# TensorE's order in the attention stage: the waits of two score groups put together, the value products behind the scores

## The reference, cut to what matters

```python
def attn(x, w_q, w_k, w_v, w_o):            # x: (16, 256, 256) f32, 16 heads of 16 features
    q, k, v = proj(w_q), proj(w_k), proj(w_v)
    scores = einsum('bhqd,bhkd->bhqk', q, k) * SCALE
    probs = softmax(scores)                 # over the 256 keys
    return einsum('bhqk,bhkd->bhqd', probs, v) ... @ w_o.T
x = layernorm(x + attn(x))
# then 8 experts, 2 for each of the 4096 tokens, at most 1280 tokens an expert:
#   gates, lists of tokens, relu(buf @ w1 + b1) @ w2 + b2, weighted sum
x = layernorm(x + ffn(x))
```

## Time and profile before

| | us |
|---|---|
| three runs | 1002.49, 996.72, 1003.08 (median 1002.49) |
| the profiled execution | 998.63 |
| its span, from the first to the last instruction | 996.9 |
| the stretch in which both score groups run in each turn | 76 to 376 |
| the experts' stretch at full work | 484 to 950 |

### The profile page before, as it was taken

The page is one execution under the profiler, slowest core; times in us unless marked ns, Lnnn a source line. Parts: engine busy times, 40 slices in busy tenths (PEclk is TensorE's granted clock), DMA queues, the critical chain, the costliest instruction groups (busy, mean ns, idle before and its releaser), DMA issues. The chain is left out here.

```text
span 996.9 us, 19588 instructions
## 1 busy us (share of the span) xinstructions
PE 841.5 (84%) x7441; PEld 754.0 (76%) x7441; DVE 560.8 (56%) x1125; ACT 460.5 (46%) x851; POOL 443.8 (45%) x674
## 2 busy tenths in 40 slices
PE   4559999999999987620699999999999999999940
PEld 4446777776777765520699999999999999999940
DVE  3345767776777774421456555456665655556415
ACT  3016656665666665201344444454444434454316
POOL 2001122555666556775334444445454444445325
PEclk9569989999999999755699999999999999999985
DMA  2967556777664640101424325233443433322229
GB/s 89 266 99 108 86 98 123 118 116 116 110 100 88 119 77 24 44 22 37 147 32 92 91 43 128 44 85 86 90 88 50 109 69 86 86 43 43 28 36 328
DMA packets 71225, 90.77 MB, mean 91 GB/s; under 512 B 10940, under 2 KB 62300, under 8 KB 71004
## 3 DMA queue, kind: packets, MB, share of 16 engines
q1 hardware_dynamic: 53724, 68.48, 31.5%
q0 software_dynamic: 17408, 21.05, 12.8%
HBM read 37.87 MB, written 25.84 MB: 64 GB/s over the span
## 5 line engine op out<-in xcount | busy, mean ns | idle before, releaser
L953 POOL DMA_INDIRECT acc_rows<-o_w,lists x80 | 136.8, 1710 | 242.6 <-ACT o_w L1004 230.4
L626 DVE TENSOR_REDUCE negm<-wide 128x4 f32<-128x1024 f32 x128 | 156.3, 1221 | 72.6 <-PE wide L728 71.0
L1082 PE MATMUL wide<-g_hi,w_hi 128*128 128x256 f32 x640 | 184.3, 288 | 0.0
L1084 PE MATMUL wide<-g_hi,w_lo 128*128 128x256 f32 x640 | 181.1, 283 | 0.0
L1083 PE MATMUL wide<-g_lo,w_hi 128*128 128x256 f32 x640 | 180.8, 283 | 0.0
L1101 PE MATMUL bank<-w_lo,h_hi 128*128 128x256 f32 x640 | 180.1, 281 | 0.0
L1100 PE MATMUL bank<-w_hi,h_hi 128*128 128x256 f32 x640 | 180.1, 281 | 0.0
L1102 PE MATMUL bank<-w_hi,h_lo 128*128 128x256 f32 x640 | 179.8, 281 | 0.0
L994 ACT ACTIVATE h<-wide,b1T 128x256 f32<-128x256 f32 x320 | 133.2, 471 | 70.8 <-DVE h_hi L1037 53.1
L473 ACT ACTIVATE probs<-wide 128x1024 f32<-128x1024 f32 x128 | 131.1, 1024 | 73.9 <-PE wide L742 70.3
L1004 ACT ACTIVATE o_w<-o_b,lists 128x256 f32<-128x256 f32 x80 | 36.3, 501 | 193.5 <-DVE o_b L1050 193.5
(11 more groups left out here) (143 smaller groups left out, 1518.3 us busy)
## 6 DMA issues: line engine op xcount, KB each, us to landing
stack<-qk SPq DMA_DIRECT2D x64, 256.0 KB, 7.1
w_raw<-in_L_ffn_w SPq DMA_DIRECT2D x16, 1024.0 KB, 5.8
stack<-qk SPq DMA_DIRECT2D x64, 128.0 KB, 5.9
x_sb<-in_L_attn_x SPq DMA_DIRECT2D x16, 256.0 KB, 4.7
x_rows<-x SPq DMA_DIRECT2D x16, 256.0 KB, 3.5
acc_rows<-x SPq DMA_DIRECT2D x16, 256.0 KB, 4.3
acc_sb<-acc_rows SPq DMA_DIRECT2D x8, 512.0 KB, 7.9
out<-out_sb SPq DMA_DIRECT2D x8, 512.0 KB, 3.7
```

What stands on the lines that cost most here:

```text
L626: nc.vector.tensor_reduce(negm[n % 2][:, :, :, u].rearrange("p c x -> p x c"), SQ[:, :, :].rearrange("p x (c t) -> p x c t", c=QC), X, ALU ...
L953: nc.gpsimd.indirect_dma_start(out=acc_d, out_offset=bass.IndirectOffsetOnAxis(ap=lists[:, e, QC * c + r, 0:1], axis=0), in_=o_w[c][:, r, ...
L1082: nc.tensor.matmul(out, w1_hi[:, k, f], G_hi[:, k, :], start=(k == 0), stop=False)
L1084: ins = nc.tensor.matmul(out, w1_lo[:, k, f], G_hi[:, k, :], start=False, stop=(k == DK - 1))
```

## The change

The waits of `scores` and `shifted_scores` become functions of their own, called one after the other in front of both groups; the value products of the turn follow right behind the two groups, ahead of `MT`, `UT`, `AT`, `X1T` and `POS`, where they stood behind these. No instruction is added or taken out, no buffer and no offset changes; the programs of the other engines are untouched.

```diff
--- before.py
+++ after.py
@@ -715,13 +715,24 @@
                     lambda i: src_hi[:, i, c * P:c * P + P], lambda i: src_lo[:, i, c * P:c * P + P],
                     lambda i: wT_hi[:, w, i, :], lambda i: wT_lo[:, w, i, :]))
 
-            def scores(n, u):
-                st, i = stack[n % SB], PAIRS * n + u
+            def scores_due(n, u):
+                i = PAIRS * n + u
                 if i == 0:
                     pe.wait_ge(b1T_done, 1)
                 if u == 0:
                     pe.wait_ge(stacked[n % SB], 128 * (n // SB + 1))
                 pe.wait_ge(max_done, i)
+
+            def shifted_scores_due(n, u):
+                i = PAIRS * n + u
+                if i == 0:
+                    pe.wait_ge(keys_ready, 16 * 2 * SB)
+                if u == 0:
+                    pe.wait_ge(shift_in, 64 * (n + 1))
+                pe.wait_ge(exp_done, i)
+
+            def scores(n, u):
+                st = stack[n % SB]
                 for c in range(QC):
                     for x in range(2):
                         k = slice(HALF * x, HALF * x + KEYS)
@@ -730,12 +741,7 @@
                 ins.then_inc(s_ready, 1)
 
             def shifted_scores(n, u):
-                st, i = stack[n % SB], PAIRS * n + u
-                if i == 0:
-                    pe.wait_ge(keys_ready, 16 * 2 * SB)
-                if u == 0:
-                    pe.wait_ge(shift_in, 64 * (n + 1))
-                pe.wait_ge(exp_done, i)
+                st = stack[n % SB]
                 for c in range(QC):
                     for x in range(2):
                         k = slice(HALF * x, HALF * x + KEYS + 2)
@@ -760,12 +766,19 @@
                 ins.then_inc(pv_ready, 1)
 
             for turn in range(LAST + 1):
-                p = pair_of(turn, S0, NB)
-                if p is not None:
-                    scores(*p)
-                p = pair_of(turn, ST0, NB)
-                if p is not None:
-                    shifted_scores(*p)
+                ahead, behind = pair_of(turn, S0, NB), pair_of(turn, ST0, NB)
+                if ahead is not None:
+                    scores_due(*ahead)
+                if behind is not None:
+                    shifted_scores_due(*behind)
+                if ahead is not None:
+                    scores(*ahead)
+                if behind is not None:
+                    shifted_scores(*behind)
+                for t in range(QUADS):
+                    m = due(turn, PV0 + 2 * t, NB)
+                    if m is not None:
+                        pv(m, t)
                 n = due(turn, MT, NB)
                 if n is not None:
                     pe.wait_ge(max_done, PAIRS * (n + 1))
@@ -814,10 +827,6 @@
                         nc.tensor.matmul(out, tri[:, :], mask[:, c, :], start=True, stop=False)
                         ins = nc.tensor.matmul(out, ones[:, :], (seen[m % 2], seen_t)[c][:, :], start=False, stop=True)
                     ins.then_inc(pos_ready, 1)
-                for t in range(QUADS):
-                    m = due(turn, PV0 + 2 * t, NB)
-                    if m is not None:
-                        pv(m, t)
                 n = due(turn, Q, NB)
                 if n is not None:
                     pe.wait_ge(xT_lo_done, n + 1)
```

## The result

| | us |
|---|---|
| the kernel before, median of 18 runs | 1002.02 (996.72 to 1009.75) |
| the changed kernel, median of 18 runs | 1010.46 (1004.96 to 1016.61) |
| ratio, with its 95% interval | 1.0081 (1.0059 to 1.0102) |
| profiled execution, before and after | 998.63 and 1014.60 |
| its span, before and after | 996.9 and 1012.8 |

The change costs 8.4 us by the two medians, 8.1 by the ratio. The two profiled executions are 16 us apart, one from the lower part of its kernel's runs and one from the upper: their stretches can't simply be subtracted.

The account below looks back on a forecast made before the run. TensorE, busy 841.5 of 996.9 us, was taken to bound the kernel. The terms 6.9 - 1.2 + 0.5 = +6.2 us, on a mean of 1000.2 us over four executions, gave 1006 us, range 997 to 1014.

Parts of the forecast that it names:

- UT behind the value products: Turn 3's eight transposes end later, delaying VectorE's division and MT in turn 4: 0.55 us a steady round, +6.9 us in all.
- POS behind them: Turn 7's four small matmuls next to V save one passage between array layouts: 0.1 us in 12 rounds, -1.2 us.
- AT behind them: Turn 5's four transposes still end before ScalarE's `aT_hi` reads them, 0.3 us to spare: cost 0, at most 0.5.
- waits in front: Both score groups' waits ahead of the scores: 0.05 to 0.1 us in ten turns, +0.5 us, bounds 0 and 2.
- The cover by the one subtraction: In turn 4 VectorE's 0.68 us `qk` subtraction before the reciprocals takes 0.45 of the 1.00 us delay; 0.55 gets through.
- The forecast wait of `MT`: Sign in turn 4: MT's wait for VectorE's line 568 grows from 0.2 to about 0.8 us in nearly every round.
- the three special rounds: Rounds outside the ten steady ones: late stack rows 0.2 us, slightly late scores 0.5, last turn 3 but one 0.7.
- The bound of 14.3: Upper bound for moving turn 3's transposes: all of the 1.02 us gets through in 14 rounds, 14.3 us.
- Nothing arrives: Rival: longer rounds give late stack rows time, so other stalls shrink by turn 4's loss; 998 to 1001 us, chance 0.15.
- Faster: Rival: the wait ahead of the shifted scores' weights was a hurdle; 0.11 us less in 117 turns, 985 to 993, chance 0.06.
- Slower by over 1%: Rival: one more wait ahead of the scores costs 0.1 us in each of 117 turns, above 1017 us, chance 0.16.
- the forecast's own range: Range of the main case: 999 to 1012 us, from 4 to 9 us on a base between 996 and 1003, chance 0.63.

Follow-up runs that it names:

- experiment 10: Kernel before with only the eight transposes of turn 3 (UT) behind the value products, on a chip without the hold: 1.0056 of the kernel before.
- experiments 6: The changed kernel unaltered, run again for a profile on the same chip as the kernel before: 1.0092 of the kernel before.
- 7: Changed kernel with only AT, the four transposes of turn 5, put back ahead of the value products: 1.0064 of the kernel before.
- experiment 11: Kernel before with only the waits of both score groups in front, value products in their old place, without the hold: 1.0052 of the kernel before.
- experiment 9: Changed kernel with UT, the transposes of turn 3, ahead of the value products again, on a chip without the hold: 1.0038 of the kernel before.
- experiment 2: Changed kernel with UT, the transposes of turn 3, ahead of the value products again, on the chip with the hold: 1.0338 of the kernel before.
- experiment 5: The kernel before unaltered, run again for a profile: 1.0007 against itself.
- experiment 1: Kernel before with only the eight transposes of turn 3 (UT) behind the value products, first chip: 0.9942 of the kernel before.
- experiment 8: Changed kernel with UT ahead of the value products and GpSimd's four list transfers one turn later, on a chip without the hold: 1.0211 of the kernel before.

## Why the prediction was right, step by step

The forecast was 1006 us with a range of 997 to 1014; 1010.5 came. By parts, on chips without the hold:

| part | forecast, us | measured, us |
|---|---|---|
| UT behind the value products | +6.9 | +5.6 (3.1 to 8.1; experiment 10) |
| POS behind them | -1.2 | turn 7 shorter by 0.09 to 0.1 in each round |
| AT behind them | 0 | not to be told from 0 (experiments 6, 7) |
| waits in front | +0.5 | +5.2 (2.4 to 8.0; experiment 11) |
| all but UT | -0.7 | +3.8 (1.0 to 6.6; experiment 9) |
| whole change | +6.2 | +8.1 (5.9 to 10.2) |

The measured ones are ratios times the median beside them. 5.6 and 3.8 make 9.4, which lies within the interval of the whole, so nothing speaks against adding the two halves.

- *UT in turn 3.* Right in place and size. The cover by the one subtraction gave way as worked out: 0.55 forecast, 0.52 measured in each steady round. The forecast wait of `MT` of about 0.8 is 0.73 in the row. Experiment 10 has it in ten rounds, as many as were counted. What the three special rounds cost can't be read beneath the late stack rows there. The bound of 14.3 was never near.
- *AT in turn 5.* Right where signals come in time: the trace of the changed kernel has the four transposes end at 267.52 and ScalarE's `aT_hi` start at 267.88, with no wait, and turn 6 keeps 3.29.

```profile
266.86 0.66 PE L702 MATMUL bank<-ident,attn 128*128 128x128 f32 x4
...
267.88 0.58 ACT L511 ACTIVATE aT_hi<-bank 128x512 fp32r<-128x512 f32 x1
```

But I called that cover 0.3 us wide and priced its loss at 0.5 at most. On the chip with the hold a kernel with the same place of `AT` (experiment 2) lost 2.3 us in turn 6 and 1.5 in turn 7 of each round. The bound was read from a trace in which signals are quick.
- *POS in turn 7.* Right: 0.1.
- *Both waits in front.* Mis-sized: +0.5 forecast within 0 to 2, +5.2 measured. The step priced each wait at the turn where it stands and found nothing, and in the steady turns that is so: the score groups stay 0.34 apart (259.30 to 259.64). Two things are missing from it. First, it said of the scores that wait for `shift_in` that TensorE loses nothing; in experiment 11 turn 86 lost 1.15 us to that wait, and turns 70 and 102 lost 0.25 each. Second, it left out that the edit changes what is issued at all, and with that turns 142 to 148, in which no scores are left. 2.5 us are found there in the mean of seven profiles, 4.7 in that of experiment 11, most of it with the lower clock. How the other 2.7 divide between the waits for the maxima, the clock elsewhere (from 76 us to the end of turn 149 it is at 1.2 GHz for 30.6 us in experiment 11, 13.6 in experiment 5 and 17.0 in the first profile of the kernel before) and what differs from run to run stays open.

The rivals. *Nothing arrives*: wrong, the steady loss is repaid nowhere. *Faster*: wrong, the shifted scores follow the scores by 0.34 us as before, so the 0.11 us are no hurdle that the order of the waits could take away. The first half of the Trainium skill's rule (TensorE: Matmul & The Clock Gate, Part 3) would have given the 13 us. With the second, that loads overlap matmuls in flight only where they go to another row group, the unchanged distance agrees; but no run had score groups on other rows, and the profile shows the loads of the shifted scores start at 259.52, while the matmuls of the scores (259.30 and 0.50, ends modelled) are in flight on the same two row groups. So whether that rule is the reason stays open. *Slower by over 1%*: its mechanism, 0.1 us a turn, is wrong, since six of eight turns kept their length; of its direction some was right, by another way. What the forecast owes to luck: UT was put 1.3 us too high and the waits 4.7 too low, and the base of four executions, 1000.2 in the mean, was 1.8 under the median of 18 runs. The errors stayed inside the range because it was made for runs that differ by more than the change. The 1% that I said a measurement can't tell was too coarse: with 18 runs of each kernel the interval is 0.2% to either side. And 4 us on a base of 996 make 1000, not the 999 at the lower edge of the forecast's own range.

## What to carry to other kernels

Ask of an edit in the order of waits not only what each wait delays but whether the waits still fit where they were: two in front of one instruction became 89 more instructions here, and most of the price that was found lay in turns that the edit does not reorder. When work moves behind other work, follow its reader to the next thing that waits for it and look for what covers it: one subtraction of 0.68 us took 0.45 of 1.00, and the rest went through one for one. And take a ratio of half a per cent on more than one chip before a sign is believed: UT alone was 0.994 on one and 1.006 on another.

## What the runs showed of the hardware that was not expected

- On one of four chips, in the hour of these runs, TensorE's signals of turn 5 came up to 2.9 us late in each round from the first list transfers on. Four kernels profiled there have it, and the three of them that ran elsewhere too had it there at most in single rounds. Whether a kernel pays hangs on what stands behind the value products: with `AT` behind them 3.4%, with `AT` ahead 0.4% or, for experiment 1, 0.6% less than the kernel before beside it. That one had no profile there; its median was 5.7 to 10.9 us above its others, so it most likely paid too, which is argued and not shown. Whether the list transfers cause the hold is open: experiment 8 would have told it on that chip.
- An issue of SyncE for an 8 KB transfer, 0.63 us as a rule, took up to 2.50, at the same place of SyncE's program in each kernel with the waits in front, though SyncE's program is the same in all. Each of the 30 issues of that line over 0.9 us ended 0.14 to 0.41 us after a piece of the program's code had landed.
- Around a wait of 1.03 us near the thin end of the stage TensorE's clock fell to 1.2 GHz for 10.2 us, and turns 142 to 148 took 17.7 us instead of 13.0. In experiment 7, on another chip, a wait of 1.06 us in the same place cost no clock (1.00 granted), and the turns took 13.95. What made the difference isn't shown.
